# Stacking the 64-channel chunk on 128 partitions in the query and output projections of an attention kernel

## What is computed

```
q       = x @ W_q                                  # 112 x 320
k_t,v_t = text @ W_k, text @ W_v                   # 371 x 320
probs   = softmax(q k_t / 4)                       # per head
text_out = probs @ v_t
qsem    = l2norm(probs @ text)                     # compared with the normalized ip rows
probs_ip = softmax(q k_ip / 4 + 0.5 * sem) * mask
out     = (text_out + probs_ip @ v_ip) @ W_out + b_out + x
```

## Time and profile before

| | |
|---|---|
| median of three runs | 756.78 us (753.31, 756.78, 757.88) |
| profiled execution, its own time | 755.47 us |
| its span | 753.7 us |
| busy share PE, DVE, ACT, POOL | 96%, 86%, 74%, 57% |
| mean granted clock of PE | 0.995 of full |

### The profile page before, as it was taken

How to read it: one execution, slowest core, us unless ns; L and a number is a source line. 1 busy time by engine, 2 the same in 40 slices (tenths; PEclk the granted TensorE clock), 3 DMA queues, 4 the chain that set the end, 5 groups by cost and what they waited for, 6 DMA issues and landing times.

```text
span 753.7 us, 22634 instructions
## 1 busy us (share of the span) xinstructions
PE 724.7 (96%) x7279; PEld 564.7 (75%) x7279; DVE 647.0 (86%) x1860; ACT 556.2 (74%) x1590; POOL 428.7 (57%) x515
## 2 busy tenths in 40 slices
PE   7799999999999999999999999999999999999887
PEld 5477778787877878778787777878777787877664
DVE  4478998989889898988989898899989889898983
ACT  5368687777868778687877878777787878777770
POOL 7245646456564655646565565556656565654653
PEclk9999999999999999999999999999999999999999
DMA  9655362541636345252534436253352624234000
GB/s 262 134 142 109 75 137 63 85 119 37 123 71 122 79 69 131 41 121 72 117 85 59 97 81 126 72 113 82 62 104 72 132 72 85 61 59 103 11 5 17
DMA packets 136195, 67.95 MB, mean 90 GB/s; under 512 B 76320, under 2 KB 136016, under 8 KB 136080
## 3 DMA queue, kind: packets, MB, share of 16 engines
q1 hardware_dynamic: 131504, 63.77, 40.0%
q10 hardware_dynamic: 4576, 2.74, 1.3%
HBM read 39.76 MB, written 15.24 MB: 73 GB/s over the span
## 4 chain that ended last, share of the span: by engine, by line
PE 64%; DVE 15%; issue 7%; POOL 4%; SPq 3%; ACT 3%; DMA 2%; POOLq 0%; DVEq 0%; ACTq 0%
PE ps_gram L742 13%; PE ps_prep L640 12%; PE ps_pT L725 10%; PE ps_gram L743 9%; PE ps_prep L696 5%; PE ps_score L717 4%; PE ps_val L751 3%; DVE pT_lo L1112 3%; DVE low L1107 2%; POOL dual L570 2%; DVE quad_junk L1125 2%; PE ps_prep L790 2%; PE ps_val L752 2%; POOL nrm L577 2%; DVE k_lo L1047 1%
## 5 line engine op out<-in xcount | busy, mean ns | idle before, releaser
L570 POOL TENSOR_TENSOR dual<-prob 128x371 f32<-128x371 f32 (+1 forms) x288 | 253.9, 882 | 295.9 <-ACT prob L940 295.8
L742 PE MATMUL ps_gram<-gram_hi,pT_hi 125*128 125x371 f16 (+1 forms) x864 | 272.3, 320 | 0.1
L743 PE MATMUL ps_gram<-gram_lo,pT_hi 125*128 125x371 f16 (+2 forms) x864 | 230.1, 267 | 0.0
L934 ACT ACTIVATE pT_hi<-ps_pT 125x384 f16<-125x384 f32 (+1 forms) x288 | 139.2, 483 | 108.4 <-PE ps_pT L725 101.6
L924 ACT ACTIVATE prob<-ps_score,low 128x371 f32<-128x371 f32 (+1 forms) x288 | 165.6, 575 | 41.4 <-DVE low L1107 37.5
L1112 DVE TENSOR_TENSOR pT_lo<-ps_pT,pT_hi 125x384 f16<-125x384 f32 (+1 forms) x288 | 155.4, 540 | 33.2 <-ACT pT_hi L934 29.0
L1107 DVE TENSOR_REDUCE low<-ps_score 128x1 f32<-128x371 f32 (+1 forms) x288 | 155.0, 539 | 20.9 <-PE ps_score L717 15.9
L725 PE MATMUL ps_pT<-ident,prob 128*125 128x128 f32 (+1 forms) x864 | 144.0, 275 | 14.3 <-DVE pT_lo L1112 7.6
L1125 DVE CUSTOM_DVE_ANT_0 quad_junk<-ps_gram,dual 128x371 f32<-128x371 f32 (+1 forms) x288 | 153.0, 531 | 3.1 <-issue 0.6
L725 PEld LDWEIGHTS ps_pT<-ident,prob 128*125 128x125 f32 (+1 forms) x864 | 128.8, 187 | 34.3 <-ACT prob L924 15.0
L751 PE MATMUL ps_val<-val,pT_hi 125*128 125x84 f16 (+3 forms) x864 | 152.3, 196 | 0.0
(11 more groups left out here) (200 smaller groups left out, 1481.2 us busy)
## 6 DMA issues: line engine op xcount, KB each, us to landing
ctx_sb<-in_ctx_t SPq DMA_DIRECT2D x15, 750.0 KB, 4.9
w_raw<-k_bounce SPq DMA_DIRECT2D x32, 216.0 KB, 3.9
k_st<-k_bounce SPq DMA_DIRECT2D x28, 216.0 KB, 3.9
k_bounce<-k_hi SPq DMA_DIRECT2D x15, 288.0 KB, 4.3
k_bounce<-k_lo SPq DMA_DIRECT2D x15, 288.0 KB, 4.2
q_st<-q_bounce SPq DMA_DIRECT2D x60, 63.0 KB, 2.5
k_st<-k_hi SPq DMA_DIRECT2D x32, 84.0 KB, 3.2
k_st<-k_lo SPq DMA_DIRECT2D x32, 84.0 KB, 3.6
```

The lines of the kernel that those rows point to most:

```text
L570: nc.gpsimd.tensor_tensor(dual[0:r, t % 2, :], prob[0:r, g % 4, 0:TX], prob_16[0:r, t % 2, :], ALU.subtract).then_inc(s_dual, 1)
L742: nc.tensor.matmul(ps_gram[t % 2][:, 0:TX], hi, gh[0:TROWS[i], i, :], start=(i == 0), stop=False, skip_group_check=True)
L743: last = nc.tensor.matmul(ps_gram[t % 2][:, i * TC:TX], hi, gl[0:TROWS[i], i, i * TC:TX], start=False, stop=(i == NT - 1), skip_group_chec ...
```

## The change

x, W_q and W_out are laid out by the host with the rows 256 to 319 twice, so that the last chunk has 128 rows, its 64 channels in the upper and again in the lower half. Each is then one DMA. In the last chunk of the query projection the weights become [hi of W; lo of W] in `wq_hi` and [hi of W; 0] in `wq_lo`, so that two matmuls do the work of three: `wq_hi` with `x_hi`, `wq_lo` with `x_lo`. In the output projection the stationary side is stacked: the last chunk of `attn_hi` is [hi; lo], `wo_hi` is [hi; hi] and `wo_lo` is [lo; 0]; again two matmuls for three, and they now stand at the end, after the wait. `attn_lo` has two chunks. SP no longer waits for POOL's zeros; ACT waits for them before it makes `wq_hi`.

```diff
-            eng.dma_start(dst[:, 0:CC - 1, 0:C], src[0:(CC - 1) * P, :].rearrange("(c p) n -> p c n", p=P)).then_inc(s, 16)
-            eng.dma_start(dst[0:CR, CC - 1, 0:C], src[(CC - 1) * P:C, :]).then_inc(s, 16)
+            eng.dma_start(dst[:, :, 0:C], src.rearrange("(c p) n -> p c n", p=P)).then_inc(s, 16)
...
-                sp.dma_start(xt_sb[a.odd][:, 0:CC - 1, :], x_t[a.n, 0:(CC - 1) * P, :].rearrange("(c p) s -> p c s", p=P)).then_inc(s_xt[a.odd], 16)
-                sp.dma_start(xt_sb[a.odd][0:CR, CC - 1, :], x_t[a.n, (CC - 1) * P:C, :]).then_inc(s_xt[a.odd], 16)
+                sp.dma_start(xt_sb[a.odd][:, :, :], x_t[a.n, :, :].rearrange("(c p) s -> p c s", p=P)).then_inc(s_xt[a.odd], 16)
...
-            sp.wait_ge(s_zero, 1)
             load_xt(start)
...
-            for x_ in xt_sb:
-                nc.gpsimd.memset(x_[:, CC - 1, :], 0.0)
-            nc.gpsimd.memset(wq_sb[:, 0:CC - 1, C:CC * P], 0.0)
-            for w_ in (wq_sb, wo_sb):
-                last = nc.gpsimd.memset(w_[:, CC - 1, :], 0.0)
-            last.then_inc(s_zero, 1)
+            nc.gpsimd.memset(wq_lo[:, CC - 1, :], 0.0)
+            nc.gpsimd.memset(wo_lo[:, CC - 1, :], 0.0)
+            nc.gpsimd.memset(wq_sb[:, :, C:CC * P], 0.0).then_inc(s_zero, 1)
...
                     for j in range(CC):
-                        last = split3(bank[:, j * S:(j + 1) * S], lambda h_, c: (wq_hi, wq_lo)[h_][:, c, j * P:(j + 1) * P],
-                                      lambda h_, c: (x_hi, x_lo)[h_][:, c, :], CC)
+                        dst, cols = bank[:, j * S:(j + 1) * S], slice(j * P, (j + 1) * P)
+                        for c in range(CC - 1):
+                            nc.tensor.matmul(dst, wq_hi[:, c, cols], x_hi[:, c, :], start=(c == 0), stop=False)
+                            nc.tensor.matmul(dst, wq_hi[:, c, cols], x_lo[:, c, :], start=False, stop=False)
+                            nc.tensor.matmul(dst, wq_lo[:, c, cols], x_hi[:, c, :], start=False, stop=False)
+                        nc.tensor.matmul(dst, wq_hi[:, CC - 1, cols], x_hi[:, CC - 1, :], start=False, stop=False)
+                        last = nc.tensor.matmul(dst, wq_lo[:, CC - 1, cols], x_lo[:, CC - 1, :], start=False, stop=True)
...
                     pe.wait_ge(s_fin_ev, NF * f.n + k)
-                    for c in range(CC):
-                        last = nc.tensor.matmul(bank[0:S, 0:C], attn_lo[:, c, :], wo_hi[:, c, :], start=False, stop=(c == CC - 1))
+                    for c in range(CC - 1):
+                        nc.tensor.matmul(bank[0:S, 0:C], attn_lo[:, c, :], wo_hi[:, c, :], start=False, stop=False)
+                    for w_ in (wo_hi, wo_lo):
+                        last = nc.tensor.matmul(bank[0:S, 0:C], attn_hi[:, CC - 1, :], w_[:, CC - 1, :], start=False, stop=(w_ is wo_lo))
...
             split_hi(start, PIECE_X)
-            split_weight(wq_hi[:, :, :], wq_sb[:, :, :], s_wq, 2)
+            act.wait_ge(s_zero, 1)
+            split_weight(wq_hi[:, :, :], wq_sb[:, :, :], s_wq, 1)
...
-                    hi, lo = (t[:, :, :].rearrange("p c s -> p (c s)") for t in (attn_hi, attn_lo))
-                    last = nc.vector.tensor_tensor(lo, bank[:, 0:CC * S], hi, ALU.subtract)
+                    rest = (CC - 1) * S
+                    hi, lo = (t[:, 0:CC - 1, :].rearrange("p c s -> p (c s)") for t in (attn_hi, attn_lo))
+                    nc.vector.tensor_tensor(lo, bank[:, 0:rest], hi, ALU.subtract)
+                    last = nc.vector.tensor_tensor(attn_hi[CR:P, CC - 1, :], bank[0:CR, rest:CC * S], attn_hi[0:CR, CC - 1, :], ALU.subtract)
...
+            def split_wq():
+                dve.wait_ge(s_wsplit_hi, 2)
+                low_part(wq_lo[:, 0:CC - 1, :], wq_sb[:, 0:CC - 1, :], W_UP, wq_hi[:, 0:CC - 1, :])
+                nc.vector.tensor_copy(wq_lo[0:CR, CC - 1, :], wq_hi[0:CR, CC - 1, :])
+                low_part(wq_hi[CR:P, CC - 1, :], wq_sb[CR:P, CC - 1, :], W_UP, wq_hi[CR:P, CC - 1, :]).then_inc(s_wsplit_lo, 1)
+
+            def split_wo():
+                dve.wait_ge(s_wsplit_hi, 4)
+                low_part(wo_lo[:, 0:CC - 1, :], wo_sb[:, 0:CC - 1, :], W_UP, wo_hi[:, 0:CC - 1, :])
+                low_part(wo_lo[0:CR, CC - 1, :], wo_sb[0:CR, CC - 1, :], W_UP, wo_hi[0:CR, CC - 1, :]).then_inc(s_wsplit_lo, 1)
```

More of the change, by code:

```diff
@@ L217, in build @@
         attn_hi = sb("attn_hi", [P, CC, S], F16)
-        attn_lo = sb("attn_lo", [P, CC, S], F16)
+        attn_lo = sb("attn_lo", [P, CC - 1, S], F16)
         out_sb = sb("out_sb", [S, C])
@@ L880, in split_hi @@
                 else:
-                    act.wait_ge(s_xt[a.odd], 32 * (a.pair + 1))
+                    act.wait_ge(s_xt[a.odd], 16 * (a.pair + 1))
                     reached(act, s_prep, NM * (a.n - 1) + PIECE_Q + 1)
@@ L1022, in body @@
                     if b.n == 0 and t == WO_STEP:
[L1023 removed]
+                        split_weight(wo_hi[:, :, :], wo_sb[:, :, :], s_wo, 1)
                     if t + 1 == GROUPS[group(t)][1]:
@@ L1236, in _ @@
             last.then_inc(s_kip, 1)
-            split_weight(1, wq_lo[:, :, :], wq_sb[:, :, :], wq_hi[:, :, :])
+            split_wq()
             for k in (PIECES_K[2], PIECES_K[0]):
@@ L1288, in body @@
                     if b.n == 0 and t == WO_STEP:
-                        split_weight(3, wo_lo[:, :, :], wo_sb[:, :, :], wo_hi[:, :, :])
+                        split_wo()
                     softly(t, 1)
@@ L1320 @@
     ip = ctx[:, TX:, :].transpose(1, 0, 2).reshape(B * NIP, E)
-    laid = {"x": x, "x_t": x.transpose(0, 2, 1), "ctx_t": ctx.transpose(0, 2, 1), "ip": ip, "ip_t": ip.T}
+    rows = np.concatenate([np.arange(C), np.arange((CC - 1) * P, C)])
+    laid = {"x": x, "x_t": x.transpose(0, 2, 1)[:, rows, :], "ctx_t": ctx.transpose(0, 2, 1), "ip": ip, "ip_t": ip.T}
     laid.update({name: inputs[name] for name in _INS})
+    for name in ("L0_xattn_W_q", "L0_xattn_W_out"):
+        laid[name] = np.asarray(inputs[name])[rows, :]
     for name, value in laid.items():
```

## The result

The changed kernel is slower by a quarter of a per cent: 757.44 us (755.93 to 760.15, 22 runs) against 755.45 us for the kernel before (752.94 to 759.3, 22 runs), ratio 1.0026, 95% interval 1.0016 to 1.0035. Its profiled execution took 758.12 us with a span of 755.3 us, against 755.47 and 753.7 us for the kernel before. The range of the prediction held the time, its direction was wrong.

What follows compares the result with a forecast made beforehand. PE bounds about 27 us of each batch, a DVE and POOL chain the other 17 us. Terms -1.9 - 0.27 + 0.1 + 0.1 - 0.3 = -2.3 us gave 753.8 us, 8 in 10 for 750.5 to 757.8.

Steps and rivals of the forecast that it cites:

- split of W_q: At the start on DVE: three operations for one, 0.15 to 0.45 us more, hidden in 0.44 us idle; cost 0.
- split of W_out: Step 10 of batch 0, on DVE: two operations instead of one, 0.1 us, hidden or not.
- Output projection: PE at the end of each batch: one matmul of 0.135 us less, 1.9 us gained over 14 batches.
- The tail's matmul: Output projection in the tail: one matmul less on PE, 0.27 us saved.
- that move costs nothing: Output projection: waiting for attn_lo after four matmuls, not six, is free; in the tail, DVE's part 2 was done before.
- Query projection: PE's query piece: three matmuls less a batch, taken as 0, bounds 0 and 2.4 us gained.
- what is late next is already late: After the query piece: DVE's rsum waits for POOL's vals, not PE, so PE's saved 0.147 us a batch gains 0.
- Rival B: PE's time counts everywhere, so the query part gains too: 2.3 us more, 751.5 us; chance 0.12.
- rival A: At the start, POOL's vip_diag clearing blocks DVE's wq_hi copy: 3.4 us lost, total 757.2 us; chance 0.14.
- Part 2 in two operations: DVE's part 2 at each batch's end: 0.08 us more, covered in 14 bodies; 0.1 us cost in one.
- Loads: Start, SP's queue: fewer issues, more bytes; +0.1 us up to W_v, -0.3 us later at W_out's second issue.
- The clock clause: PE's clock below full after step 6's longer wait would upset the forecast; waits of about 1 us had not lowered it.

Runs made afterwards that it cites:

- e3: Changed kernel with POOL's vip_diag clearing moved behind the split of W_q and W_out's low part made in one operation; 752.92 us, 0.9969 of the kernel before.
- e4: e3 with the old output projection: nine matmuls and attn_lo in one operation; 752.64 us, 0.9961 of the kernel before.
- e6: e3 with DVE's nrm and the two stages behind it made one step later; 750.37 us, 0.9952 of the kernel before, five executions.
- e10: Kernel before the change, with nrm and the stages behind it one step later; 754.3 us, 0.9999 of the kernel before.
- e5: e3 with three more matmuls in the query piece, 27 again, written to an unused part of its bank; 752.91 us, 0.9986 of the kernel before.
- e7: e6 with 27 query matmuls; 752.85 us, 0.9988 of the kernel before.
- e9: e3 with one tiny memset more on DVE ahead of the split of W_out; 754.22 us, 0.9986 of the kernel before.
- e1: Changed kernel, but POOL clears vip_diag only after DVE's split of W_q; 755.35 us, 0.9998 of the kernel before.
- e8: e3 with x, W_q and W_out loaded in two DMAs each, same bytes; 751.52 us, 0.9975 of the kernel before.
- e11: Kernel before the change, with one tiny memset more on DVE at step 10 of batch 0; 754.59 us, 0.9996 of the kernel before.
- e2: Changed kernel with W_out's low part made in one DVE operation again; 754.63 us, 0.9992 of the kernel before.

## Why the prediction was wrong

The direction failed at the terms that the sum put at nothing: the split of W_q (0 forecast, 3 us measured), the split of W_out (in no term of the sum, 2.2 us in the profiled execution) and a last body 1.1 us longer. The period gained about twice the forecast, and that hid part of the loss, which is luck for the range.

**Output projection, -1.9 us over 14 batches: right.** One matmul of 0.135 us forecast, 0.11 us a batch measured (e3 against e4). ACT's wait for PE at the end of step 17 was the right row to read.

**The tail's matmul, -0.27 us: not shown.** The last stretch is 0.48 us shorter in the changed kernel's trace, but the clock rose during it, and it depends on the clock more than on the edit. Where the clock stayed at 1.00 the stretch takes 4.41 us in e3 and 4.36 us in e6 with eight matmuls, and 4.38 us in e10 with nine. The step "that move costs nothing" is what fails there. It took the four matmuls at 0.27 us each, the price at the lower clock. At 0.135 us they are done before DVE's second operation, and PE waits, as the timeline of e3 shows (742 to 746 us):

```profile
743.55 0.39 DVE L1208 TENSOR_TENSOR attn_lo<-ps_prep,attn_hi 128x224 f16<-128x224 f32 x1 [1.21 <-ACT attn_hi L960]
743.96 0.27 DVE L1209 TENSOR_TENSOR attn_hi<-ps_prep,attn_hi 64x112 f16<-64x112 f32 x1
744.28 0.18 PEld L793 LDWEIGHTS ps_prep<-wo_hi,attn_lo 128*112 128x112 f16 x2 [0.27 <-DVE attn_hi L1209]
```

**Query projection, 0 forecast, 0.125 to 0.15 us a batch measured (e5, e7): wrong.** This is the step "what is late next is already late". `rsum` did wait for POOL's `vals` and not for PE, as it says, and this held up to the start of `nrm`. But the prediction followed DVE no further than `rsum`. From `nrm` on DVE depends on PE again, first through POOL's `dual` and the lock, then through ACT's `pT_hi`. Rival B had the size right, not the reason: it was no better order on DVE, the chain itself moved.

The Trainium skill ("SBUF — State Buffer", "Who interferes with whom") says that a DVE instruction with two inputs in SBUF contends with a POOL instruction that reads SBUF. The trace agrees: `nrm` takes 0.18 us ahead of `dual` (e3's last body) and 0.50 to 0.83 us when it starts behind it (e3's batches, e5, e9), ending with it.

**Split of W_q, 0 forecast, 3.0 us measured (3.21 against 0.24 us for the copy in e1; 2.1 us in the time): wrong, and named as rival A.** The copy's price was bounded by 0.15 and 0.45 us, rows in which nothing held the engine, and I let the copy of 12 elements speak against the block. That copy was not blocked here either, 0.18 us inside the clearing, while the one of 64 x 384 was. So the row with the same engine and the same neighbour was not near enough. Which difference spares the small copy, its size or its gaps, no run here shows. In the changed kernel's trace 2.0 us of the 3 show, since W_v landed earlier there.

The rule of the Trainium skill that the prediction quotes, that a copy and a POOL instruction exclude each other, agrees with the trace for a clearing too: 3.21 and 3.72 us for a copy of 0.24 us. The same section of the Trainium skill's "SBUF — State Buffer" says that a DVE instruction with two inputs in SBUF does not contend with one that only writes. The trace agrees here as well: the operation of 128 x 768 took 0.94 us inside the clearing and 0.95 us in e1 ahead of it.

**Split of W_out, "0.1 us, hidden or not", and in no term of the sum: wrong.** It cost 0.71 us and, in the profiled execution, 1.49 us more by the clock. The row that I did not ask for was what POOL does in those two microseconds: one DVE operation gets ahead of `dual` as a whole, the second of two meets it.

**Part 2 in two operations, 0.1 us: right as far as it went.** The second operation costs DVE 0.28 us, not 0.08, and was hidden in the bodies of e3 but for the 0.02 us that the output projection's 0.11 us lacks of 0.135. That the room it used up, 0.60 to 0.31 us, was room that something else needed, is the 1.0 us of the last body. The gaps in DVE's stream, 0.4 us in the batches and the start of that 1.0 us, stood in no row ahead of the prediction and in no rival.

**Loads, +0.1 and -0.3 us: not resolved.** W_v was issued 1.7 us earlier and landed 1.3 us earlier in the changed kernel's trace, but e8 and the scatter of 2 us among the one-load kernels leave no gain that can be told, and with two loads it landed at 15.09 us in e10 and e11, 1.2 us ahead of the earlier trace rows. The load of the context of batch 2 was issued at 41.80 us, 1.4 us later than in the earlier trace rows, and landed at 48.90 us, 2.0 us later. The forecast was 46.6 us.

**The sum.** Forecast -2.3 us. With the measured sizes: -3.5 us for 13 batches, +0.4 us for gaps, +2.0 start, +2.2 W_out, +1.1 last body, -0.5 end, makes +1.7 us, the +1.6 us of the two spans but for rounding. The medians say +2.0 us, about 0.7 us of it outside the span, for which the prediction had no term. (Its own range of terms, -4.0 to -1.0 us, doesn't follow from its bounds: with the loads at their best and at their worst they give -3.6 and -1.4 us.) The clock clause at the prediction's end ("waits of about 1 us did not lower it before") was of use: it was a wait of 2.00 us behind which it fell.

## What to carry to other kernels

A matmul saved in a stretch that another engine bounds can still pay in full: follow the bounding engine for several operations and ask of each input whose time it carries, locks included, before writing zero. An operation that is split in two meets its neighbours differently; look at what the other engine starts in between, and put a long clearing where no copy runs beside it. When a gain goes missing in stretches that the change doesn't touch, compare the idle times put down to nothing: one instruction more on an engine moved about 1.4 us of the span here (0.4 us in the periods and 1.0 us in the last body), and no rewriting of the work would have found it. And compare the time outside the span too, which differed by 0.8 us between kernels.

## What the runs showed of the hardware

- A DVE copy of 64 x 384 16-bit elements from SBUF to SBUF, 0.24 us alone, took 3.21 and 3.72 us beside a POOL memset of 4.36 us, and ended 0.1 us behind it. A copy of 128 x 12 elements ran in 0.18 us inside the same memset.
- DVE's place in its instruction stream: with 1879 instructions three idle times of 0.25 to 0.28 us stood before the same instructions in three kernels (the changed one, e1, e9), with 1878 none of them in six (e2, e3, e5 to e8). The time outside the span was 2.5 to 2.6 us in the first three and 2.1 us in four of the six. Why, stays open.
- The same wait of 2.00 us on PE, in two kernels with the same work around it, was followed by a granted clock of 0.59 and 0.56 in one and of 1.00 in the other. A wait of 1.29 us was followed by 1.00 in the kernel before and in e2.
- The landing of one 640 KB load, with nothing changed ahead of it in the queue, differed by 2.0 us between nine traces (14.05 us in e1 to 16.07 us in e6). The first score of these two came at 29.59 and 31.65 us.
